# One-hot matmuls that take embedding tables as fp32, one a chunk, in place of two on rounded halves (DLRM tower, Trainium2, one core)

## The reference

```python
e = jnp.stack([tbl_0[ids[:, 0]], ..., tbl_25[ids[:, 25]]], axis=1)            # 512 x 26 x 128
combined = jnp.concatenate([dense_features[:, None, :], e], axis=1)            # 27 features
interactions = jnp.einsum('bfd,bgd->bfg', combined, combined)                  # per batch row
z = jnp.concatenate([dense_features, interactions[:, iu, ju]], axis=1)         # 128 + 351
h = jnp.concatenate([z, dense_features], axis=1)                               # 607
h = jnp.maximum(h @ W_top1 + b_top1, 0.0)                                      # 512
h = jnp.maximum(h @ W_top2 + b_top2, 0.0)                                      # 256
y = h @ W_top3                                                                 # 1
```

## Time and profile before

| | |
|---|---|
| median of 3 runs (lowest to highest) | 156.84 us (154.53 to 157.45) |
| profiled execution, and its span | 156.5 us, 154.7 us |
| PE matmuls busy | 117.9 us, 76% |
| PE weight loads busy | 98.9 us, 64% |
| VectorE busy | 74.1 us, 48% |
| ScalarE busy | 73.0 us, 47% |
| GpSimd busy | 68.4 us, 44% |
| one-hot matmuls (L542, L545) | 72 + 72 records, 30.0 + 29.1 us busy |
| `tab_hi` and `tab_lo` (L360, L450) | 9.5 us on ScalarE, 10.9 us on VectorE |

### The profile page before, as it was taken

One profiled execution on the slowest core, in us unless ns is written; L12 is line 12 of the kernel. 1 busy time (PEld: TensorE's weight loads), 2 busy tenths in 40 slices (PEclk: granted clock), 3 DMA queues, 4 the chain that ended last, 5 costly groups with the idle time before them and its releaser, 6 DMA issues.

```text
span 154.7 us, 2685 instructions
## 1 busy us (share of the span) xinstructions
PE 117.9 (76%) x1038; PEld 98.9 (64%) x1038; DVE 74.1 (48%) x153; ACT 73.0 (47%) x160; POOL 68.4 (44%) x75
## 2 busy tenths in 40 slices
PE   0689999985979967550595728489929989799994
PEld 0446776662756856540394628478829989798993
DVE  3499999999999960407204510030505020237000
ACT  6795994995897820426104522002505313236211
POOL 2648072260345747474447465446456474100000
PEclk9999999999999999776559997865985799999999
DMA  5828765487961011111112121111121111100000
GB/s 156 222 71 267 207 190 110 160 221 199 354 181 42 17 51 38 34 51 34 39 44 52 28 63 32 49 34 38 34 51 33 39 50 25 27 6 0 4 0 1
DMA packets 6304, 12.58 MB, mean 81 GB/s; under 512 B 2545, under 2 KB 3157, under 8 KB 6163
## 3 DMA queue, kind: packets, MB, share of 16 engines
q1 hardware_dynamic: 3971, 7.68, 17.2%
q0 software_dynamic: 2176, 4.46, 10.9%
q10 hardware_dynamic: 144, 0.26, 0.8%
HBM read 11.27 MB, written 0.00 MB: 73 GB/s over the span
## 4 chain that ended last, share of the span: by engine, by line
DMA 34%; PE 27%; POOL 24%; issue 13%; DVE 1%; ACT 1%
DMA rows<-in_tbl_dram,ids_i 31%; POOL rows L343 24%; PE ps L603 12%; PE ps L574 7%; PE ps L525 2%; PE ps L616 2%; DMA ids_i<-in_ids_dram 2%; PE ps L558 2%; DVE z L488 1%; PE ps L626 1%; PE ps L624 1%; ACT emb_t L403 0%; DVE h_t L497 0%; ACT y L430 0%
## 5 line engine op out<-in xcount | busy, mean ns | idle before, releaser
L343 POOL DMA_INDIRECT rows<-in_tbl_dram,ids_i x68 | 67.6, 994 | 63.0 <-DMA rows<-in_tbl_dram,ids_i 45.2
L461 DVE TENSOR_SCALAR hot<-ps,row_no 125x512 fp32r<-125x512 f32 x54 | 36.6, 739 | 1.0 <-PE ps L512 1.0
L488 DVE COPY z<-ps 32x112 f32<-32x112 f32 (+1 forms) x64 | 16.5, 258 | 34.9 <-PE ps L574 22.7
L574 PE MATMUL ps<-emb_t 128*64 128x52 f32 x512 | 23.6, 251 | 11.8 <-issue 8.3
L574 PEld LDWEIGHTS ps<-emb_t 128*64 128x64 f32 x512 | 21.1, 166 | 14.8 <-issue 11.3
L542 PE MATMUL ps<-hot,tab_hi 125*128 125x512 f32 x72 | 30.0, 416 | 0.8 <-issue 0.8
L411 ACT COPY z<-ps 32x112 f32<-32x112 f32 (+1 forms) x64 | 15.2, 238 | 30.8 <-PE ps L574 19.7
L545 PE MATMUL ps<-hot,tab_lo 125*128 125x512 f32 x72 | 29.1, 404 | 0.7 <-DVE tab_lo L450 0.7
L558 PE MATMUL ps<-ident,rows 128*128 128x128 f32 x68 | 12.0, 304 | 15.2 <-DMA rows<-in_tbl_dram,ids_i 9.7
L558 PEld LDWEIGHTS ps<-ident,rows 128*128 128x128 f32 x68 | 8.3, 153 | 18.3 <-DMA rows<-in_tbl_dram,ids_i 11.7
L542 PEld LDWEIGHTS ps<-hot,tab_hi 125*128 125x128 f32 x72 | 14.1, 196 | 5.5 <-issue 2.4
(11 more groups left out here) (44 smaller groups left out, 92.7 us busy)
## 6 DMA issues: line engine op xcount, KB each, us to landing
tab<-in_tbl_dram SPq DMA_DIRECT2D x9, 448.0 KB
rows<-in_tbl_dram,ids_i POOLq DMA_INDIRECT x68, 4.6
w_fold<-w_pair SPq DMA_DIRECT2D x1, 1024.0 KB
w<-in_W_top_dram SPq DMA_DIRECT2D x1, 512.0 KB, 5.1
tab<-in_tbl_dram SPq DMA_DIRECT2D x9, 52.0 KB
x_rows<-in_r_dense_features_dram ACTq DMA_DIRECT2D x1, 256.0 KB, 3.2
w_x<-in_W_top_dram SPq DMA_DIRECT2D x1, 256.0 KB
h_t<-in_W_top_dram SPq DMA_DIRECT2D x1, 256.0 KB
```

The costliest lines, as they stand in the source:

```text
L343: pool.indirect_dma_start(out=rows[:, t, gathered.index(f), :], out_offset=None, in_=tables[f - 1], in_offset=bass.IndirectOffsetOnAxis(id ...
L461: nc.vector.tensor_scalar(hot[0:RP, k % OHB], ps[0:RP, IDV + n % 2, :], row_no[0:RP, c:c + 1], None, ALU.is_equal).then_inc(hot_dve, 1)
L488: last = nc.vector.tensor_copy(dst, src)
L574: last = nc.tensor.matmul(ps[32 * q:32 * (q + GT), bank, col:col + GC], emb_t[:, t, b0:b0 + GT, :].rearrange("p b f -> p (b f)"), emb_t[:, ...
```

## The change

Table chunks go to PE as they are, in fp32, with one-hot matrices in fp32: one matmul a chunk in place of two. The two halves, their buffers and semaphores go. The room goes to a third table buffer (`RAW` 2 to 3) and a longer ring of one-hot matrices (`OHB` 10 to 16). A table's buffer is free once its eight matmuls are done (`hot_used`), where before it was free once `tab_lo` was made. The broadcast of the ids of table n+2 moves from behind the last chunk of table n to before its seventh. GpSimd's part isn't touched.

```diff
-    OHB = 10
-    RAW = 2
-    SPLIT = 2
+    OHB = 16
+    RAW = 3
...
-        tab_hi = sb("tab_hi", [P, SPLIT, R8, D], F32R)
-        tab_lo = sb("tab_lo", [P, SPLIT, R8, D], F32R)
-        hot = sb("hot", [P, OHB, B], F32R)
+        hot = sb("hot", [P, OHB, B])
...
-                    sp.wait_ge(lo_ready, n - RAW + 1)
+                    sp.wait_ge(hot_used, (n - RAW + 1) * R8)
...
-            def split_hi(n):
-                act.wait_ge(tab_in[n], 32)
-                if n >= SPLIT:
-                    act.wait_ge(hot_used, (n - SPLIT + 1) * R8)
-                nc.scalar.copy(tab_hi[0:RP, n % SPLIT], tab[0:RP, n % RAW]).then_inc(hi_ready, 1)
...
-            def split_lo(n):
-                dve.wait_ge(hi_ready, n + 1)
-                nc.vector.tensor_tensor(tab_lo[0:RP, n % SPLIT], tab[0:RP, n % RAW], tab_hi[0:RP, n % SPLIT].bitcast(F32),
-                                        ALU.subtract).then_inc(lo_ready, 1)
...
-                    pe.wait_ge(hi_ready, n + 1)
+                    pe.wait_ge(tab_in[n], 32)
                     bank = ps[:, ROT + bank_of(s), :]
                     for c in range(R8):
+                        if c == R8 - 2 and n + 2 < NH:
+                            broadcast_ids(n + 2)
...
-                        one_hot = hot[0:RP, (n * R8 + c) % OHB]
-                        nc.tensor.matmul(bank, tab_hi[0:RP, n % SPLIT, c], one_hot, start=c == 0, stop=False)
-                        if c == 0:
-                            pe.wait_ge(lo_ready, n + 1)
-                        nc.tensor.matmul(bank, tab_lo[0:RP, n % SPLIT, c], one_hot,
-                                         start=False, stop=c == R8 - 1).then_inc(hot_used, 1)
-                    if n + 2 < NH:
-                        broadcast_ids(n + 2)
+                        nc.tensor.matmul(bank, tab[0:RP, n % RAW, c], hot[0:RP, (n * R8 + c) % OHB],
+                                         start=c == 0, stop=c == R8 - 1).then_inc(hot_used, 1)
```

More of the change, by code:

```diff
@@ L203, in dlrm_tower @@
         ids_bc_act = sem("ids_bc_act")
-        hi_ready = sem("hi_ready")
-        lo_ready = sem("lo_ready")
         hot_dve = sem("hot_dve")
@@ L385, in store_hot @@
                                ps[:, ROT + bank_of(s), :].rearrange("p (t b) -> p t b", t=T)).then_inc(stored_act, 1)
-            split_hi(0)
             build_hots(0)
-            split_hi(1)
             for s in steps:
@@ L395, in _ @@
                     store_hot(s)
-                    if n + 2 < NH:
-                        split_hi(n + 2)
                 elif s[0] == "group" and stored_by_act(s):
@@ L455, in build_hots @@
                 for m, c in enumerate(DVE_CHUNKS):
-                    if m == 2:
-                        split_lo(n)
                     k = n * R8 + c
```

## The result

| | before | after |
|---|---|---|
| median (lowest to highest) | 156.59 us (154.53 to 157.45, 4 runs) | 171.0 us (169.1 to 173.27, 4 runs) |
| ratio, 95% interval | | 1.093 (1.075 to 1.111): slower |
| profiled execution, its span | 156.5, 154.7 us | 173.27, 171.4 us |

The profiled execution of the changed kernel was the slowest of its four runs.

What follows compares the result with a forecast made beforehand. It took the chain of gathers as most of the span, with PE and gathers reaching the last rows together. 30.5 - 6.3 - 4.3 - 3.3 = +16.6 on 156.5 us gave 173 us, range 160 to 178.

Steps and rivals of the forecast that it cites:

- The matmul's price: One-hot matmuls: an fp32 one of 512 columns takes 0.893 us, four times a 128-column one.
- lower bound of 0.853: One-hot matmuls: 512 columns in fp32 with nothing but the columns, 4 x 512 / 2.4 GHz = 0.853 us.
- The rival of half rate: One-hot matmuls: one fp32 costs what two float32r ones do, 0.43 us; time 153 to 157 us; 4 in 100.
- The stage of the tables: PE's one-hot matmuls up to the first gram unit: its start moves from 57.4 to 87.9 us, +30.5.
- The middle: PE from the first gram unit to the last gathered rows: three savings, -6.3, -4.3 and -3.3 us.
- Waits for rows gone: PE's three waits for gathered rows after the tables (3.57, 1.98, 0.77 us) disappear: -6.3 us.
- Gram units: Tile 2's slow unit now comes after the last gather; half of 3.8 + 2.8 us is saved: -3.3.
- the other term: A half-clock stretch behind tile 2's slow gram unit would save 2.8 us, half of it counted within the -3.3.
- The clock: Two 1.2 GHz stretches after idle time, PE busy 3.0 and 5.6 us, return to 2.4 GHz: -4.3 us.
- The gathers: GpSimd: without `tab_lo` three long gathers lose 3.2 us of excess, the last comes before 131; neither matters to the time.
- The tail: PE and its waits from the last gathered rows to the end: 21.1 us, untouched by the change.
- slow gram units: Units beside gathers, cause unknown, left slow: 6.5 us each in tile 0, 5.9 in tile 2, against 2.1 in the last tile.
- the rival on the other side: Every gram unit takes 2.1 us, so PE catches up with the gathers: about 155 us; 9 in 100.

Runs made afterwards that it cites:

- e3: Changed kernel with the two broadcast matmuls put back behind a table's last chunk: 168.2 us, 1.083 of before.
- e4: Changed kernel without the gathers of tiles 1 to 3, PE transposing tile 0's rows in their place: 155.7 us.
- e9: Kernel before without the gathers of tiles 1 to 3, PE transposing tile 0's rows in their place: 127.0 us, 0.809 of before.
- e7: Changed kernel with two extra SBUF-to-SBUF VectorE operations a table, two-input subtractions in even tables, one-input copies in odd ones: 172.0 us in one run.
- e8: Kernel before without `tab_lo` and its matmul, one float32r matmul a chunk: 156.1 us, 0.996 of before.
- e5: Changed kernel with plain DMAs from GpSimd for the rows of tiles 1 to 3, same sizes, groups and pauses: 156.3 us, 1.002 of before.
- e6: Changed kernel with plain DMAs for the rows of tiles 1 to 3 from SyncE's queue, behind the weights: 176.1 us, 1.128 of before.
- e10: Kernel before with GpSimd issuing a group's first gather before it waits for the group before: 178.3 us, 1.150 of before.
- e1: Changed kernel with GpSimd waiting at each group for the group before last, not the last one: 217.3 us.
- e2: Kernel before with GpSimd waiting at each group for the group before last, not the last one: 195.5 us.

## Why the prediction was right, point by point

**The matmul's price: right in kind, a little high.** 0.893 forecast; 0.890 measured over six matmuls with the restart of the stream, but 0.86 in the stream itself, near the lower bound of 0.853. The 128-column matmuls that I scaled from cost 0.223 us, and a quarter of 0.86 is 0.215, so the price doesn't grow with the columns alone. The Trainium skill's FP8 and Floating Point Precision, TensorE Precision Notes, gives true fp32 four passes; the trace agrees, 0.86 us against 0.213 for 512 columns at 2.4 GHz. The rival of half rate (4 in 100) is out: a matmul's two records take 0.43 us each, not 0.43 together.

**The stage of the tables: right in sum, and its parts cancel a little.** 87.9 forecast, 87.47 measured, +30.0 us. Waits for the bank ahead of tables 2 to 6 are 0.67, 0.67, 0.66, 0.68 and 0.90 us, forecast 0.7; e3 shows them by their removal. The 69.5 matmuls at 0.86 in place of 0.893 took 2.4 us less than forecast. Against that, the slow pace at the start lasted until 14.3 and not 12.6, one matmul more at 1.7 us (+0.8), and each of the twelve breaks in the stream (seven broadcasts, five groups) cost 0.1 us more, as the first record behind a break takes 0.53 in place of 0.43 (+1.2). The profile gives a granted clock of 1.00 for that start, so that it is the 1.2 GHz level is read from the pace alone (0.853 us a record). e4 against e9, 28.5 us between their traces, measures the stage's price with no gather behind it.

**The middle: the sum right, its parts not all.** It was forecast to shrink by 13.9 us and shrank from 76.2 (57.42 to 133.62) to 62.9 (87.47 to 150.33), by 13.3. Waits for rows gone: -6.3 forecast, -6.9 in fact, since I had overlooked a fourth wait of 0.53 us at 75.13. Gram units: -3.3 forecast with the other term, 32.0 - 27.0 = 5.0 measured for the units alone, since the last one came after the last gather and took the whole 3.8, and the first was 1.9 shorter. The clock: -4.3 forecast, but what is left over is 13.3 - 6.9 - 5.0 = 1.4. That step failed in its form. The middle before has five stretches at 1.2 GHz, and I let the two go that had waits for rows ahead of them. They went, and the one from 115.2 to 121.8 too, but the one behind tile 0's units grew from 10.2 us (70.7 to 80.9) to 20.3. Ahead of it PE was busy for 1.76 of 3.4 us (96.2 to 99.6) in the slow units, and a wait of 2.09 us for VectorE begins with it. A stretch at that place comes without gathers beside it too (e4, 6.8 us), so the slow units can answer for its length at most, and no run shows even that by itself. That the sum came out is in part luck: the terms for the clock and the units missed by 3 and 2 us, one each way.

**The gathers: right in kind, half in size.** No gather over 1.1 us is left, and e7 shows why. Before, a fourth one was a little longer, which I hadn't counted (1.04 us at 19.68). The last one was forecast before 131 and came at 129.59, but the gain is 1.4, not 3.2 us, since waits for landed rows grew from 45.2 to 46.7 us in sum. The first is 4.78 us in place of 1.86. The likely reason is that three tables and `w_x` are now all issued by 4.7 us and land beside it, where before `w_x` went out at 10.6; no run separates it. As forecast, this counts for nothing: PE reaches the last rows 20 us later.

**The tail: right.** 171.4 - 150.33 = 21.1.

**The total.** By the spans, +16.7 us against +16.6 forecast, is closer than the prediction deserves, since the profiled execution lies 2.3 us above the median of the changed kernel. By the medians the change costs 14.4 us, and the forecast of 173 is 2 us too high. The other three runs had a higher mean granted clock (0.939 to 0.960, this one 0.930), so the stretches at 1.2 GHz in the middle are the likely place of the difference; no trace of them was kept.

**What was costed from one row and not understood: slow gram units.** I left them slow, "What makes them slow the trace doesn't show". They are slow because of indirect gathers: fast with none (e4, e9), fast with plain DMAs of the same sizes from GpSimd or SyncE (e5, e6), slower still with less pause (e10). In all eleven units beside gathers of the two traces the end comes 1.1 to 2.3 us after GpSimd is through with the last gather of a group (after: 90.83 to 92.10, 97.34 to 98.62, 106.72 to 109.03, 113.30 to 115.06, 130.54 to 131.75), as if the unit had to wait for the pause. In e8 one unit ends 0.4 us before that point (60.88, 61.24), so it is no strict rule. This is also what the rival on the other side hung on: with fast units the changed kernel takes 156.3 (e5), where it said 155.

**Why 14 us and not 29.** The kernel before waits for gathers whatever PE does (e8: half of the one-hot matmuls left out gives nothing). The first part of what the change adds to PE fills those waits. e9, without gathers in three tiles, shows what they cost the kernel before: 29.6 us. In the changed kernel they cost 15.3 (e4; by the lowest times 29.4 and 16.4). The difference, 13 to 14 us, is what PE's added work was hidden by: in the traces 6.9 us of waits for rows and 5.0 of slow units that now lie behind the gathers or got shorter.

## What to carry to other kernels

Two float32r matmuls on halves of a value (2 x 0.228 us for 512 columns) cost PE about half of one fp32 matmul (0.86), so that splitting pays as long as other engines have time for the halves; here VectorE and ScalarE had it. Before you cheapen the work of an engine, look whether it then reaches a wait that nothing moves (e8), and before you count added work in full, look for the waits that it fills. In this kernel the pauses between indirect gathers were worth more than they cost (e1, e2, e10): try any change of them with a look at PE's work beside them, not at the gathers' own end.

## What the runs showed that I had not expected

Indirect gathers on GpSimd hold up PE. With full pauses it costs a gram unit up to 4.4 us (6.5 in place of 2.1); with gathers every 1.25 us and hardly a pause the kernel goes from 156 to 195 us (e2) or from 171 to 217 (e1), and eight one-hot matmuls, 7 us of work, take 55 until the bank is stored (41.54 to 96.54). ScalarE's store alone isn't slower then (1.01 us), nor is a gather. Plain DMAs with the same groups and sizes do nothing of the kind (156.3 us).

Not settled: by what means. The transfers are ruled out (e5, e6), and loads of instructions are as many with fast units as with slow ones (8 packets on their queue, e5 and the changed kernel). PE's records name nobody that it waits for, and they run ahead of its completions: before, the 64 records of the first gram unit are over at 59.7, and VectorE's copy out of it starts at 63.95; the gaps in the records come behind that, as if too much were under way by then. Whether the matmuls themselves are late or their signals was not tried; that a gram unit has only one signal, at its end, speaks for the matmuls, but doesn't show it. Also open is why one-hot and first-layer matmuls beside gathers with full pauses keep their pace (5.34 us for six from 28.16 on, with four gathers from 28.78 on), while gram units, with 64 short matmuls and as many weight loads, don't.
